# A state space layer with a mixture of experts on one core: a ring of nine products for GpSimd, row scatters spread over four states, and expert rows added into the output itself

## What is computed

```python
x = L0_attn_x                                  # (8, 512, 256)
mod = (_silu(L0_c) @ L0_wmod).reshape(8, 6, 1, -1)
sa, ca, ga, sb, cb, gb = (mod[:, i] for i in range(6))
# ga, gb: sign kept, magnitude at least 0.25
h = _layernorm(x) * (1 + ca) + sa
x = x + ga * attn(h)                           # below
h = _layernorm(x) * (1 + cb) + sb
x = x + gb * ffn(h)                            # below

# attn: xn = rms(h) * norm_w;  xi, z = split(xn @ W_in);  xc = silu(conv4(xi) + conv_b)
#   dt, B, C = split(xc @ W_x);  dt = softplus(dt @ W_dt + b_dt)
#   state[s] <- exp(dt * A[s]) * state[s] + (dt * xc) * B[s]     for 16 states s, along 512 steps
#   y = sum_s state[s] * C[s] + D_skip * xc;   h + (y * silu(z)) @ W_out
# ffn: the two best of eight scores x @ Wg, weights by softmax of the two;
#   for each chosen expert: relu(normed @ W1 + b1) @ W2 + b2 + x, summed with the weights
```

## Time and profile before

| | |
|---|---|
| median of 3 runs | 1634.65 us (1633.17 to 1641.21) |
| the profiled execution | 1636.39 us, of which its span 1634.1 |
| busy, share of the span | PE 81%, DVE 76%, POOL 65%, ACT 48% |
| POOL's products (line 873) | 512, 650.9 us busy |
| VectorE's scans (line 1974) | 512, 612.0 us busy |
| row scatters on POOL (line 791) | 64, 63.9 us busy |
| late adds on POOL (line 860) | 59, 92.3 us busy |
| chain that ended last | PE 41%, DVE 20%, POOL 15%, issue 11%, ACT 8%, DMA 2% |
| granted clock of PE | 0.911 in the mean |

### The profile page before, as it was taken

One profiled execution on the slowest core, in us unless ns is written; L12 is line 12 of the kernel. 1 busy time (PEld: TensorE's weight loads), 2 busy tenths in 40 slices (PEclk: granted clock), 3 DMA queues, 4 the chain that ended last, 5 costly groups with the idle time before them and its releaser, 6 DMA issues.

```text
span 1634.1 us, 25818 instructions
## 1 busy us (share of the span) xinstructions
PE 1329.9 (81%) x7954; PEld 1081.0 (66%) x7954; DVE 1237.3 (76%) x2161; ACT 786.4 (48%) x1378; POOL 1054.4 (65%) x942
## 2 busy tenths in 40 slices
PE   4567786777777887887888788778799999999994
PEld 1245465455556665665666566767689999999993
DVE  3798999989979889889998987789355555555552
ACT  2666768757857766775776586476000000000000
POOL 2485887998797898889789687978324352212221
PEclk7797998998989989889888988889999999999997
DMA  6212131321233344334144132944957797667664
GB/s 224 68 52 76 51 56 53 110 74 57 91 103 104 89 145 110 99 112 139 66 120 143 43 108 97 260 149 130 332 158 201 205 270 206 203 201 200 204 185 138
DMA packets 129471, 221.83 MB, mean 136 GB/s; under 512 B 17052, under 2 KB 74920, under 8 KB 129080
## 3 DMA queue, kind: packets, MB, share of 16 engines
q1 hardware_dynamic: 110376, 186.34, 37.3%
q0 software_dynamic: 16064, 28.53, 7.2%
q10 hardware_dynamic: 2896, 5.31, 1.1%
HBM read 182.79 MB, written 41.54 MB: 137 GB/s over the span
## 4 chain that ended last, share of the span: by engine, by line
PE 41%; DVE 20%; POOL 15%; issue 11%; ACT 8%; DMA 2%; SPq 1%; DVEq 0%; POOLq 0%; ACTq 0%
PE psum L1673 12%; PE psum L1689 12%; POOL dBu L873 10%; DVE w_sb L1974 10%; PE psum L1491 5%; DVE y L1985 3%; PE psum L1500 2%; ACT psum L1125 2%; POOL gT L727 2%; POOL rows_d L791 2%; PE psum L1629 2%; ACT hc L1109 1%; PE psum L1642 1%; PE psum L1480 1%; DVE xc L1955 1%
## 5 line engine op out<-in xcount | busy, mean ns | idle before, releaser
L873 POOL TENSOR_TENSOR dBu<-w_sb,brep 128x512 f32<-128x512 f32 x512 | 650.9, 1345 | 65.4 <-DVE w_sb L1974 54.1
L1974 DVE TENSOR_TENSOR_SCAN w_sb<-psum,dBu 128x512 f32<-128x512 f32 x512 | 612.0, 1210 | 93.8 <-ACT psum L1125 46.0
L1491 PE MATMUL psum<-ident,w_sb 128*128 128x128 f32 x2048 | 312.0, 301 | 153.2 <-DVE y L1985 101.1
L1125 ACT ACTIVATE psum<-w_sb,aneg 128x512 f32<-128x512 f32 x512 | 347.6, 692 | 179.3 <-DVE w_sb L1974 176.4
L1491 PEld LDWEIGHTS psum<-ident,w_sb 128*128 128x128 f32 x2048 | 253.3, 154 | 232.2 <-DVE y L1985 144.3
L860 POOL DMA_INDIRECT sum_d<-dBu,token x59 | 92.3, 1564 | 307.7 <-DVE dBu L2196 286.1
L1109 ACT ACTIVATE hc<-psum,ct 128x512 f32<-128x512 f32 x256 | 174.7, 682 | 114.8 <-PE psum L1491 87.4
L1500 PE MATMUL psum<-ident,hc 128*128 128x128 f32 x1024 | 178.1, 308 | 47.8 <-ACT hc L1109 36.4
L1500 PEld LDWEIGHTS psum<-ident,hc 128*128 128x128 f32 x1024 | 138.5, 159 | 92.3 <-ACT hc L1109 62.9
L1985 DVE SCALAR_TENSOR_TENSOR y<-psum,ct,y 128x512 f32<-128x512 f32 x240 | 174.2, 726 | 14.1 <-PE psum L1491 13.7
L1673 PE MATMUL psum<-xgT,win 128*128 128x128 f32 x960 | 112.2, 275 | 1.8 <-issue 1.8
(11 more groups left out here) (264 smaller groups left out, 1758.2 us busy)
## 6 DMA issues: line engine op xcount, KB each, us to landing
brep<-b_d SPq DMA_DIRECT2D x128, 256.0 KB, 3.6
win<-in_W SPq DMA_DIRECT2D x30, 1024.0 KB, 5.0
expert_pieces<-in_W SPq DMA_DIRECT2D x29, 1024.0 KB, 5.0
expert_pieces<-in_W SPq DMA_DIRECT2D x42, 512.0 KB, 5.2
dBu<-rows_d SPq DMA_DIRECT2D x35, 257.0 KB, 2.8
w_sb<-in_W SPq DMA_DIRECT2D x8, 1024.0 KB, 12.9
xg<-rows_d SPq DMA_DIRECT2D x22, 257.0 KB, 2.8
h_d<-hmod SPq DMA_DIRECT2D x8, 512.0 KB, 2.9
```

Source lines behind the costliest of these rows:

```text
L873: nc.gpsimd.tensor_tensor(dBu[:, i % RING, :], u[p][:, c, :], brep[:, s % 4, :], ALU.mult).then_inc(s_dBu, 1)
L1125: nc.scalar.activation(dA[:, i % DA_RING, :], dt[p][:, c, :], ACT.Exp, scale=aneg[:, c, s:s + 1]).then_inc(s_dA, 1)
L1491: last = nc.tensor.transpose(T[:, i // DT, c * P:(c + 1) * P], hs[s % 2][:, c, i * P:(i + 1) * P], ident[:, :])
L1974: nc.vector.tensor_tensor_scan(hs[s % 2][:, c, :], dA[:, i % DA_RING, :], dBu[:, (n * UNITS + i) % RING, :], 0.0, ALU.mult, ALU.add).then_ ...
```

## The change

- `RING` is 9 instead of 6.
- The row scatters of sequence n-2 move: choice 0 to s=0 and s=1 of body n (were s=15 of the body before and s=0), choice 1 to s=4 and s=5 (were s=1 and s=2). In the epilogue all eight of sequence 6 come after the last `gate`.
- `tile_out(t-1)` moves from s=4 to s=6 on POOL. On SP, `load_gate` moves from s=6 to s=9, and `tile_rows` with `tile_pieces` of tile 0 from s=6 to s=7 in sequence 3.
- sum_d goes. The base is stored into `out`, the tiles' rows are added into `out`, with a bounds check that drops the rows of padding. The zeroed spare rows and the eight copies at the end go with it; at the end SP waits only for the adds and the stores of the base.

```diff
-RING = 6
+RING = 9
-    sum_d = dram("sum_d", (NTOK + P, D))
-        def store_out(eng, n):
-            eng.dma_start(out[n * L:(n + 1) * L, :].rearrange("(p i) d -> p (i d)", p=P),
-                          sum_d[n * L:(n + 1) * L, :].rearrange("(p i) d -> p (i d)", p=P)).then_inc(s_out, 16)
...
-                sp.dma_start(rows(sum_d, n), x1[:, :, :]).then_inc(s_bast, 16)
+                sp.dma_start(rows(out, n), x1[:, :, :]).then_inc(s_bast, 16)
...
-                sp.wait_ge(s_const, 1)
-                sp.dma_start(sum_d[NTOK:NTOK + P, :], zrow).then_inc(s_zero, 16)
...
-                    if 3 <= n <= 6 and s == 6:
+                    if 3 <= n <= 6 and s == (7 if n == 3 else 6):
                         tile_rows(t)
                         tile_pieces(t, (0, 1, 2))
-                    if n >= 1 and s == 6:
+                    if n >= 1 and s == 9:
                         load_gate(n - 1)
...
                 sp.wait_ge(s_st, 16 * TILES)
-                for n in range(0, NB, 2):
-                    store_out(sp, n)
-                sp.wait_ge(s_out, 16 * NB)
+                sp.wait_ge(s_bast, 16 * NB)
...
-                pool.indirect_dma_start(sum_d, bass.IndirectOffsetOnAxis(ap=idx[:, t % 2:t % 2 + 1], axis=0),
-                                        ysb[:, :], None, compute_op=ALU.add).then_inc(s_st, 16)
+                pool.indirect_dma_start(out, bass.IndirectOffsetOnAxis(ap=idx[:, t % 2:t % 2 + 1], axis=0),
+                                        ysb[:, :], None, bounds_check=NTOK - 1, oob_is_err=False, compute_op=ALU.add).then_inc(s_st, 16)
...
-                pool.indirect_dma_start(sum_d, bass.IndirectOffsetOnAxis(ap=token[:, i % XR:i % XR + 1], axis=0),
-                                        ysl[:, i % YR, :], None, compute_op=ALU.add).then_inc(s_st, 16)
+                pool.indirect_dma_start(out, bass.IndirectOffsetOnAxis(ap=token[:, i % XR:i % XR + 1], axis=0),
+                                        ysl[:, i % YR, :], None, bounds_check=NTOK - 1, oob_is_err=False, compute_op=ALU.add).then_inc(s_st, 16)
...
                     if n >= 2 and s == 0:
+                        send_rows(n - 2, 0, (0, 1))
+                    if n >= 2 and s == 1:
                         send_rows(n - 2, 0, (2, 3))
-                    if n >= 2 and s == 1:
+                    if n >= 2 and s == 4:
                         send_rows(n - 2, 1, (0, 1))
-                    if n >= 2 and s == 2:
+                    if n >= 2 and s == 5:
                         send_rows(n - 2, 1, (2, 3))
...
-                    if 4 <= n <= 7 and s == 4:
+                    if 4 <= n <= 7 and s == 6:
                         tile_out(t - 1)
...
-                    if has_o and s == 15:
-                        send_rows(n - 1, 0, (0, 1))
...
                 tile_out(BEGIN - 1)
-                send_rows(NB - 2, 0, (2, 3))
                 gate(NB - 1, 1)
+                send_rows(NB - 2, 0)
                 send_rows(NB - 2, 1)
...
-                act.wait_ge(s_zero, 16)
...
-                act.wait_ge(s_st, 16 * TILES)
-                for n in range(1, NB, 2):
-                    store_out(act, n)
```

More of the change, by code:

```diff
@@ L81, in adaln_kernel, with program @@
         YT = psum[:, 4:8, :]
-        program(nc, ctx, sem, ident, tab, psum, T, dA, Q, MOD_PS, YT, mod_d, b_d, h_d, rows_d, sum_d, out,
+        program(nc, ctx, sem, ident, tab, psum, T, dA, Q, MOD_PS, YT, mod_d, b_d, h_d, rows_d, out,
                 x, norm_w, W_in, conv_w, conv_b, W_x, W_dt, b_dt, A_log, D_skip, W_out, Wg, cT, wmod,
                 gamma, beta, W1, b1, W2, b2)
-def program(nc, ctx, sem, ident, tab, PS, T, dA, Q, MOD_PS, YT, mod_d, b_d, h_d, rows_d, sum_d, out,
+def program(nc, ctx, sem, ident, tab, PS, T, dA, Q, MOD_PS, YT, mod_d, b_d, h_d, rows_d, out,
             x, norm_w, W_in, conv_w, conv_b, W_x, W_dt, b_dt, A_log, D_skip, W_out, Wg, cT, wmod,
@@ L205, in program @@
         m8n = gT[0:NB, 0, 0:2 * D].rearrange("p (a d) -> p a d", a=2)
-        zrow = hc[:, 0, 0:D]
         def two_of(t):
@@ L212, in program @@
         xs_of = [xin[:, :, :], two_of(xc)[0], *two_of(u), *two_of(dt), *two_of(sz)]
-        s_zero = sem("spare_rows_zeroed")
         s_w = sem("weights_loaded")
@@ L330, in program @@
         s_yb = sem("late_tile_y_with_bias")
-        s_out = sem("out_stored")
         X0_PS = PS[:, 0:4, :]
@@ L657, in _ @@
         def _(pool):
-            pool.memset(zrow, 0.0)
             pool.memset(mhalf[:, :], -0.5)
@@ L999, in store_base @@
                 act.wait_ge(s_base, n + 1)
-                act.dma_start(sum_d[n * L:(n + 1) * L, :].rearrange("(i p) d -> p i d", p=P), x1[:, :, :]).then_inc(s_bast, 16)
+                act.dma_start(out[n * L:(n + 1) * L, :].rearrange("(i p) d -> p i d", p=P), x1[:, :, :]).then_inc(s_bast, 16)
             def mod_copy(j):
```

## The result

The changed kernel takes 1621.36 us in the median of 14 runs (1618.43 to 1633.70), beside 1634.21 us for 14 runs of the kernel before: ratio **0.9928**, 95% interval 0.9907 to 0.9948, so some 12 us faster. Timed once more in a later set it took 1621.77 against 1640.42: 0.9879, 0.9844 to 0.9914. The forecast was 25.9 us; just under a half of it came in the first timing, some three quarters in the second. Its time lies 0.4 us above the upper end of the range.

A forecast was written before the change was run, and what follows sets the result against it. VectorE, with POOL right behind, bounds the recurrence, PE the expert tiles, and unhidden copies the last 16.6 us. Savings 16.2 + 5.3 + 4.3 + 1.2 - 1.1 = 25.9 us from 1634.65 give 1608.8 us, range 1598 to 1621.

The forecast's parts named there:

- The copy: End of the kernel: copies from sum_d to out vanish, 16.2 us saved of 16.6, some 0.4 staying for closing the program.
- The bounds check: Adds of expert rows into the output: cost taken as 0, with -2 to +2 us allowed for the last two adds.
- Rival D: Slower: bounds check done row by row in POOL's software, gain gone at 3.3 us extra per add; chance 0.04.
- n=2 and n=3: Recurrence, third product of s=3: fewer scatters ahead of POOL's products save 5.3 us in n=2 and 4.3 in n=3.
- n=4 to 6: Recurrence: n=5 saves 1.2 us, n=4 and n=6 nothing, as delays of ACT and PE cover most; bounds 0 and 3.5.
- I give the ring of nine itself nothing at these stalls: Recurrence: POOL's start in s=15 waits for ACT or the table, not ring space, so the deeper ring saves 0.
- The price I gave this: Scatter pairs beside VectorE's residual sums in s=4 and s=5: n=7 alone loses some 1.0 us more, two sums at 0.5 each.
- n=7: Sequence 7: tile_out(7) moved to s=6 makes VectorE wait 3.9 us for its landing; 1.1 us lost net.
- The cover of half a us: n=7, tile 9's rows and weights reach PE with half a us to spare; costed at nothing, up to 3 us for the range.
- The late tiles: Expert tiles after the recurrence: PE sets the pace and hides the adds, so no change, 0 us.
- Rival C: Later scatters come too late in n=3 and n=7, eating 10 us; only the copy's gain remains: 1618.5 us; chance 0.25.
- Rival B: Ring and spread let POOL run further ahead, covering most of VectorE's 26.4 us of stalls: 1592 to 1600 us; chance 0.17.

The follow-up runs named there:

- copy_only: Changed kernel with the ring of six and every old place, leaving only the rows added straight into the output: 1626.34 against 1640.79 us, ratio 0.9918.
- psum_resid: Changed kernel, ring of nine, with the gated product left in its PSUM bank so the residual addition reads one SBUF tensor: 1606.52 us, ratio 0.9798.
- best9: Changed kernel, ring of nine, with the gated product left in PSUM and the tile's add of n=7 back in state 4: ratio 0.9822.
- ring6: Changed kernel with RING = 6: 1618.38 us, ratio 0.9865 to the kernel before.
- ring9_only: Kernel before with RING = 9 and nothing else: 1660.52 us, ratio 1.0117.
- old9_psum: Kernel before with RING = 9 and the gated product of the residual left in PSUM: ratio 0.9982.
- out4: Changed kernel with the tile's add of n=7 back in state 4: 1616.78 us, ratio 0.9850 to the kernel before.

## Why the prediction was off

**The copy (16.2 us forecast): right, by a us too large.** 15.1 us by the traces, 13.5 (9.7 to 17.2) as timed in copy_only. I left 0.4 us after the last add's landing. But the last add landed 2.7 us after its issue, at about 1614.1, and the end came 3.1 us later, not within 1 us as the text had it: what ends last is GpSimd's closing DRAIN, 5.85 us long in both kernels, at 1616.99. Before, it ran behind the copies. From the last issue to the end it is 5.84 us now (1611.36 to 1617.2) where I had 3.75 + 0.4.

**The bounds check (0): right.** 29 ns and 5 ns. Rival D falls: the adds are still hidden behind PE's tile, and from issue to next issue it is 3.57 us at the end. POOL itself waited longer for the add before, 35.6 us in 7 waits against 15.8 in 4 (15.1 in 4 in copy_only, with the same check), but no other engine waited for a late add.

**n=2 and n=3 (5.3 and 4.3 saved): right by the waits, and by the two profiles of after.** In the profiles n=2 is 6.0 and 5.1 us shorter and n=3 5.5 and 4.6; the third product of s=3 still comes 1.89 and 1.87 us late, as the working said (about 1.8, and under 2.5). Part of n=2's gain in the first profile is PE's clock, 0.93 against 0.88. How much time it gives is less sure than that: in psum_resid and best9, with the same places, n=2 took 134.9 and 134.6 us at 0.82 and 0.83 and n=3 138.2 and 138.7, where before took 135.5 and 140.8. VectorE's waits for POOL had shrunk there too (in psum_resid to 3.8 us in the two sequences), but it waited longer for ACT.

**n=4 to 6 (1.2 saved): wrong, and this is the step that failed.** They grew by 3.8 and 2.6 us, so 4 to 5 us against the sum (and by 6 to 8 against the 414.1 of copy_only), and n=6 (+2.7 and +2.4) by more than the 2 us from which the text called itself wrong. The step is the sentence "I give the ring of nine itself nothing at these stalls", and with it that n=4 and n=6 were put at nothing. For the stalls that was so; but I asked only what a longer lead can give and not what POOL does with it. Where it has more free buffers it fills more without a break, and VectorE pays when its residual addition falls into that run. The three additions grew from 5.95 us to 16.39: 4.35 of the 10.4 came with the new places of the scatters, 6.1 with the ring (ring6). In the old places the ring costs 19 us (ring9_only), and old9_psum gives 22 back, which ties nearly all of it to the addition.

**The price I gave this.** I had a part of the mechanism in hand, from the earlier trace rows and the sentence of the Trainium skill (GPSIMD Engine Reference, Key points) that GpSimd's SBUF interfaces are shared with VectorE, and sized it by one product's slowdown of a quarter of 2.05 us, in n=7 alone. By that the two additions there cost 1.0. Both the size and the place were wrong. The earlier trace rows show POOL waiting for one long instruction of VectorE; the other way about the residual addition waits for the rest of a whole *run* of POOL's, of up to fourteen products, which no row I had picked shows. The rows to pick were the additions of n=4, 5 and 6 in the trace of before: 1.98, 1.98 and 1.99 us, and 0.69 everywhere else but in n=7 (1.74). In n=7, to which I gave the loss, the first takes 1.57 us in the changed kernel and the second 0.69, less than before, since a moved pair of scatters ends POOL's run there. The Trainium skill (SBUF — State Buffer, SBUF: two separate sides) says that the pair is locked for the whole instruction; the traces agree in that POOL's fourth product stood still behind VectorE's long instruction in the earlier trace rows (7.00 us for four instead of 4.95). They show more: between POOL's products, queued back to back, the residual addition was not let in, in any of the 29 cases in which two or more products ran beside it. But that is no rule for every instruction with two SBUF inputs. The long ones of line 1964, in the kernel before:

```profile
L1964 DVE TENSOR_TENSOR w_sb<-w_sb,xc x4: 2257/2260/2262, 183.4 to 997.5; 128x2048 f32<-128x2048 f32 x4
L1964 DVE TENSOR_TENSOR w_sb<-w_sb x3: 2257/2258/2698, 308.3 to 859.3; 128x2048 f32<-128x2048 f32 x3
```

The one of the earlier trace rows is the 2698 ns: it took 0.44 us more than the 2.26 of the others, to the end of the product that ran when it started, and was done at 311.04, before the run of four ended at 312.16. It was let in ahead of the fourth product. Why this one was and the short addition never was, no run here tells.

**n=7 (1.1 lost): the mechanism right, the sum short.** The add was forecast to be issued some 41 us after the start of the sequence and was at 40.7; the wait forecast at 3.9 us is 4.38. The cover of half a us for tile 9's rows and weights, costed at nothing and at 3 us for the range, was gone as well: out4 shows it at 4.67 us of PE's waiting. In the changed kernel it hides mostly behind the other wait, and state 6 is reached 2.1 us later than before, at 64.0 against 61.9. From there to the first late tile the changed kernel loses another 2.6, or nothing in the second profile; in the epilogue POOL issues eight scatters after the last gate where it was four (and two ahead of it: so two more before the first late add, not four more, as the text had it), with one wait of 5.95 us for the landing of the first four. In all +4.7 and +2.0.

**The late tiles (0)** took 3.2 us more in one profile and 0.1 in the other; among the kernels here that stretch runs from 435.5 to 439.6 without an order that follows an edit. That stays open.

By terms, the first profile: -15.1 at the end, -11.5 in n=2 and 3, +3.8 in n=4 to 6, +4.7 in n=7, +3.2 in the late tiles, -2.2 in n=0 and 1, +0.2 ahead of them: -16.9, from 1634.1 to 1617.2. The timed medians differ by 12 to 13 us in the same set; the profiled execution of the changed kernel, 1619.02, lies under its median of 1621.36, that of before, 1636.39, above its 1634.21. Rival C (1618.5) is nearest to the time, but only part of it for its reason: the late transfers cost 2 to 5 us in n=7 and nothing in n=3. The larger part has no rival of mine. Rival B asked for the lead to pay; it did the reverse.

## What to carry to other kernels

A buffer ring is a licence to run on: before it is deepened, look up in the trace which instructions of VectorE read two SBUF tensors and stand where POOL will now be working without a break, and allow for each up to the rest of that run, not only its own length. Add what starves behind it: here PE idled through the wait and came back at half its clock. The cure is small where one of the two inputs can stay in PSUM (here some 13 us for an edit of a few lines), and the sign to look for is one group whose instructions of the same shape have two durations. Where work is moved later, count every consumer of what it produces: taking away the first that waited showed the second here.

## What the runs showed of the hardware

An addition of two SBUF tensors of 128x512 takes 0.69 us on VectorE when POOL makes no products, and 1.6 to 6.9 us beside a run of POOL's products, ending 0.55 to 0.57 us after the last of them in all 34 cases. Reading one operand from PSUM, it takes 0.69 us everywhere. An instruction of 128x2048 with two SBUF inputs was let in between two products and held the next one up for 2.05 us, so two SBUF inputs alone do not tell how long an instruction waits.

POOL's products lose nothing that the traces show beside the addition. The run of six there is recorded as 7.98 us against 7.40 elsewhere, but the 0.6 belongs to the tile's add in front of it: four products behind such an add, with no addition beside them, take 5.51 us instead of 4.95 (before, at 686.48):

```profile
685.40 1.62 POOL L852 DMA_INDIRECT sum_d<-ysb,idx  x1 [0.16 <-issue]
686.48 5.51 POOL L873 TENSOR_TENSOR dBu<-w_sb,brep 128x512 f32<-128x512 f32 x4
```

An indirect add into DRAM with a bounds check costs what one without it does, within 5 ns in the median, and the DRAIN at the end of GpSimd's program takes 5.85 us.
